# Quantised rows rounded before they are transposed, and laid out by two engines instead of one

## The reference, cut to what matters

```python
def _layernorm(x, axis=-1, eps=1e-05):
    m = jnp.mean(x, axis=axis, keepdims=True)
    v = jnp.var(x, axis=axis, keepdims=True)
    return (x - m) / jnp.sqrt(v + eps)

def fake_quant(x, n_bits=N_BITS):
    qmax = 2 ** (n_bits - 1) - 1
    scale = jnp.maximum(jnp.max(jnp.abs(x)) / qmax, 1e-08)
    q = jnp.clip(jnp.round(x / scale), -qmax - 1, qmax) * scale
    return x + jax.lax.stop_gradient(q - x)

qkv = jnp.einsum('bnc,oc->bno', fake_quant(x), fake_quant(w_qkv)) + b_qkv      # x: the normalised rows
attn = jnp.einsum('bhnd,bhmd->bhnm', fake_quant(q), fake_quant(k)) * scale
```

## Time and profile before

| | value |
|---|---|
| median of three runs | 2032.84 us (2028.87 to 2034.92) |
| span of the profiled execution | 2037.3 us |
| busy: TensorE, VectorE, ScalarE, GpSimd | 74%, 70%, 68%, 57% |
| start of `normalise`'s loop, its last reduction | about 299 us, 423 us |

### The profile page before, as it was taken

One profiled execution on the slowest core, in us unless ns is written; L12 is line 12 of the kernel. 1 busy time (PEld: TensorE's weight loads), 2 busy tenths in 40 slices (PEclk: granted clock), 3 DMA queues, 4 the chain that ended last, 5 costly groups with the idle time before them and its releaser, 6 DMA issues. The chain is left out here.

```text
span 2037.3 us, 49150 instructions
## 1 busy us (share of the span) xinstructions
PE 1498.2 (74%) x12152; PEld 991.7 (49%) x12153; DVE 1431.0 (70%) x3551; ACT 1376.4 (68%) x3956; POOL 1162.3 (57%) x1903
## 2 busy tenths in 40 slices
PE   6999957856656565663688885888865999994663
PEld 6999954411111111111344443555534988884553
DVE  2544559978777777776466666888876777774896
ACT  1323224429999999997799994777753766663885
POOL 2333330046666666662455552677775888884997
PEclk9999978955555555555555555555556999997786
DMA  7654310002222222221544445444433555554785
GB/s 293 258 231 193 160 39 1 1 32 83 85 75 76 76 87 75 84 78 49 136 138 150 143 146 152 132 154 154 154 123 107 140 140 137 146 144 143 224 271 159
DMA packets 184974, 263.32 MB, mean 129 GB/s; under 512 B 28372, under 2 KB 147363, under 8 KB 180328
## 3 DMA queue, kind: packets, MB, share of 16 engines
q1 hardware_dynamic: 137456, 202.16, 31.8%
q0 software_dynamic: 19840, 39.17, 5.4%
q10 hardware_dynamic: 27540, 20.52, 3.1%
HBM read 149.17 MB, written 108.01 MB: 126 GB/s over the span
## 5 line engine op out<-in xcount | busy, mean ns | idle before, releaser
L956 ACT ACTIVATE exps_summed<-s,neg_shift 128x197 f32<-128x197 f32 x1184 | 481.9, 535 | 32.4 <-POOL neg_shift L830 30.4
L956 ACT ACTIVATION_READ_ACCUMULATOR exps_summed<-s,neg_shift (+1 forms) x1184 | 339.0, 317 | 0.0
L993 DVE TENSOR_REDUCE score_max<-s 128x788 f32 (+3 forms) x320 | 285.9, 893 | 66.5 <-PE s L900 58.7
L1353 ACT ACTIVATE exps<-st,scalars 128x788 f32<-128x788 f32 (+1 forms) x320 | 246.4, 891 | 17.6 <-PE st L1262 17.5
L2034 POOL DMA_INDIRECT expert_sums<-y_tile,row_places x216 | 218.4, 1011 | 60.9 <-issue 28.9
L384 PE MATMUL mm<-w_tok,x_transposed 128*128 128x192 f32 x1176 | 209.4, 328 | 0.8 <-ACT x_transposed L345 0.8
L345 ACT COPY x_transposed<-tp 128x768 f32<-128x768 f32 x98 | 78.1, 798 | 176.8 <-PE tp L376 176.8
L384 PEld LDWEIGHTS mm<-w_tok,x_transposed 128*128 128x128 f32 x1176 | 190.8, 192 | 1.2 <-ACT x_transposed L345 1.2
L367 POOL TENSOR_SCALAR x_patches<-x_tile 128x768 f32<-128x768 f32 x98 | 81.4, 831 | 187.7 <-PE tp L376 172.1
L1173 POOL TENSOR_SCALAR probs<-exps 128x788 bf16<-128x788 f32 (+1 forms) x160 | 130.0, 819 | 102.3 <-ACT exps L1353 100.7
L900 PE MATMUL s<-k_int,qk_int 16*128 16x197 bf16 x768 | 98.7, 354 | 108.8 <-ACT exps_summed L956 106.0
(11 more groups left out here) (416 smaller groups left out, 4531.9 us busy)
## 6 DMA issues: line engine op xcount, KB each, us to landing
x_tile<-in_x SPq DMA_DIRECT2D x21, 1792.0 KB, 11.1
z_tile<-listed_rows SPq DMA_DIRECT2D x108, 196.0 KB
v_ints<-v_slots SPq DMA_DIRECT2D x32, 480.0 KB
v_slots_in<-v_ints SPq DMA_DIRECT2D x32, 480.0 KB, 3.6
q_ints<-qk_int SPq DMA_DIRECT2D x32, 295.5 KB
k_ints<-k_int SPq DMA_DIRECT2D x32, 295.5 KB
q_shifted<-q_ints SPq DMA_DIRECT2D x32, 295.5 KB, 3.6
k_ones<-k_ints SPq DMA_DIRECT2D x32, 295.5 KB, 4.3
```

The lines of the kernel that those rows point to most:

```text
L956: act.activation(gone[:, w % 2, k], ps[(turn + w) % 3][:, k, 0:SEQ], ACT.Exp, scale=alpha, bias=nb[:, s, to:to + 1], accum_out=p.lsum[:, b ...
L993: dve.tensor_reduce(columns(m, u), src, op=ALU.max, axis=AXL.X).then_inc(max_done, 1)
L1353: act.activation(ex[:, v % 4, 0:size(u)], src, ACT.Exp, scale=alpha, bias=p.col(C_LNSA)).then_inc(e_ready, 1)
```

## The change

GpSimd gets the rounding: it reads `y` and writes `yr` (`y_rounded`, bf16, two buffers), so TensorE transposes bf16 with the bf16 identity, and PSUM holds bf16. The two parts of a token now go to separate banks: channels 0 to 127 to `pa` as before, channels 128 to 191 to the bank `maxima` in even turns and to the fifth bank of `pq` in odd turns. What is left is plain copies: ScalarE lays out the first part of every turn and the last part of even turns, VectorE the last part of odd turns. ScalarE copies turn t - 2 behind the normalisation of turn t. The doubles and the reductions are the same.

```diff
-        pa = [p.ps(f"pa{k}", [128, 4, 128], F32, c) for k in range(2)]
+        pa = [p.ps(f"pa{k}", [128, 8, 128], BF16, c) for k in range(2)]
...
+        def turned_to(x, rows, t):
+            first = 1 + 4 * t
+            return x[0:rows, :, first:first + 4].rearrange("p b (u e) -> p b u e", e=2)
+
+        def first_channels(t):
+            return pa[t % 2][:, 0:2, :]
+
+        def last_channels(t):
+            b = pq[:, 4] if t % 2 else bank[:]
+            return b[0:D1].bitcast(BF16)[:, 0:2 * ROWS].rearrange("p (u n) -> p u n", u=2)
...
-                for t in range(NG * SIDE // 2):
-                    need(act, t_done, t - 1)
+                def copies(t):
+                    act.wait_ge(t_done, t + 1)
+                    act.copy(turned_to(x0, 128, t), by_image(first_channels(t))).then_inc(x0_act, 1)
+                    if t % 2 == 0:
+                        act.copy(turned_to(x1, D1, t), by_image(last_channels(t))).then_inc(x1_act, 1)
+
+                for t in range(TURNS):
+                    need(act, r_ready, t - 1)
                     for u in range(2):
...
                     ins.then_inc(y_ready, 1)
+                    if t >= 2:
+                        copies(t - 2)
+                copies(TURNS - 2)
+                copies(TURNS - 1)
...
                 pool.wait_ge(ones_ok, 1)
+                for t in range(TURNS):
+                    pool.wait_ge(y_ready, t + 1)
+                    need(pool, t_done, t - 1)
+                    pool.tensor_scalar(yr[:, t % 2], y[:, t % 2], MAGIC, MAGIC, ALU.add, ALU.subtract).then_inc(r_ready, 1)
...
-                    pe.wait_ge(y_ready, t + 1)
-                    need(pe, x_ready, t - 1)
+                    pe.wait_ge(r_ready, t + 1)
+                    need(pe, x0_act, t - 1)
+                    need(pe, x1_dve if t % 2 else x1_act, t // 2)
                     for u in range(2):
-                        nc.tensor.transpose(pa[b][:, u, 0:ROWS], y[:, b, u, 0:128], p.idf[0:ROWS, 0:ROWS])
-                        done = nc.tensor.transpose(pa[b][0:D1, 2 + u, 0:ROWS], y[:, b, u, 128:D], p.idf[0:ROWS, 0:ROWS])
+                        nc.tensor.transpose(first_channels(t)[:, u], yr[:, b, u, 0:128], p.idb[0:ROWS, 0:ROWS])
+                        done = nc.tensor.transpose(last_channels(t)[:, u], yr[:, b, u, 128:D], p.idb[0:ROWS, 0:ROWS])
...
-                        need_apart(pe, x_ready, 7 * (g + 1), tick_t)
-                    need_apart(pe, q_max, ND * g + d - 1, tick_t)
+                        turns = (SIDE // 2) * (g + 1)
+                        pe.wait_ge(x0_act, turns)
+                        pe.wait_ge(x1_act, (turns + 1) // 2)
+                        pe.wait_ge(x1_dve, turns // 2)
+                    need(pe, q_max, ND * g + d - 1)
...
-                def spread(g, w2):
...
-                    for dst, src, rows in ((x0, pa[b][:, 0:2, :], 128), (x1, pa[b][0:D1, 2:4, :], D1)):
-                        first = 1 + 2 * SIDE * g + 4 * w2
-                        ins = dve.tensor_scalar(dst[0:rows, :, first:first + 4].rearrange("p b (u e) -> p b u e", e=2),
-                                                src.rearrange("p u (b e) -> p b u e", e=2), MAGIC, MAGIC, ALU.add, ALU.subtract)
-                    ins.then_inc(x_ready, 1)
+                def odd_turn(t):
                     dve.wait_ge(t_done, t + 1)
+                    dve.tensor_copy(turned_to(x1, D1, t), by_image(last_channels(t))).then_inc(x1_dve, 1)
```

More of the change, by code:

```diff
@@ L441, in normalise @@
         y = p.sb("y", [ROWS, 2, 2, D], F32, c)
+        yr = p.sb("y_rounded", [ROWS, 2, 2, D], BF16, c)
         cy = p.sb("class_y", [128, D], F32, c)
@@ L445, in normalise @@
         mx = p.sb("qkv_max", [128, NG, 5, PAIRS], F32, c)
-        pa = [p.ps(f"pa{k}", [128, 4, 128], F32, c) for k in range(2)]
+        pa = [p.ps(f"pa{k}", [128, 8, 128], BF16, c) for k in range(2)]
         pq = p.ps("pq", [128, 5, 512], F32, c)
         bank = p.ps("maxima", [128, 512], F32, c)
[L449 to L452, removed]
+        (ld, chain, chain_a, red, w_t, w_ok, b_in, b_mv, y_ready, r_ready, t_done, x0_act, x1_act, x1_dve, cls_t,
+         q_done, q_max, red2, eps_ok, max_ok, rows_ok, ones_ok) = p.sems(
+            p.early, "b", "ld chain chain_a red w_t w_ok b_in b_mv y_ready r_ready t_done x0_act x1_act x1_dve cls_t "
+            "q_done q_max red2 eps_ok max_ok rows_ok ones_ok")
         DOUBLES = ([((q, j), (q, j + 1)) for q in range(PAIRS) for j in (0, 2)]
@@ L464, in normalise, with by_image @@
         cw1 = p.cw1
+        TURNS = NG * SIDE // 2
+        def turned_to(x, rows, t):
[6 more added lines that the diff above has]
+            return b[0:D1].bitcast(BF16)[:, 0:2 * ROWS].rearrange("p (u n) -> p u n", u=2)
+        def by_image(v):
+            return v.rearrange("p u (b e) -> p b u e", e=2)
         p.cw0 = cw0
@@ L644, in _ @@
                 dve.sem_inc(w_ok, 1)
-                def spread(g, w2):
-                    t = g * (SIDE // 2) + w2
-                    b = t % 2
+                def odd_turn(t):
                     dve.wait_ge(t_done, t + 1)
-                    for dst, src, rows in ((x0, pa[b][:, 0:2, :], 128), (x1, pa[b][0:D1, 2:4, :], D1)):
-                        first = 1 + 2 * SIDE * g + 4 * w2
-                        ins = dve.tensor_scalar(dst[0:rows, :, first:first + 4].rearrange("p b (u e) -> p b u e", e=2),
-                                                src.rearrange("p u (b e) -> p b u e", e=2), MAGIC, MAGIC, ALU.add, ALU.subtract)
-                    ins.then_inc(x_ready, 1)
+                    dve.tensor_copy(turned_to(x1, D1, t), by_image(last_channels(t))).then_inc(x1_dve, 1)
                 def maxima(g, d):
@@ L664, in _ @@
                     for w2 in range(SIDE // 2):
-                        spread(g, w2)
+                        t = g * (SIDE // 2) + w2
+                        if t % 2:
+                            odd_turn(t)
                         if g:
```

## The result

The changed kernel takes 2078.6 us, median of four runs (2070.86 to 2079.33); the kernel before took 2033.0 on the same chip. The ratio is 1.0222 [1.0202, 1.0242]: slower by 45.6 us, where 10 us faster was predicted and 2032 was the upper end of the range.

What follows compares the result with a forecast made beforehand. VectorE was taken to bound the edited stage. Steady part -12.6, fill +1.5, clock +2.7 and end -2 sum to -10.4 us from the median 2032.84: 2022.4 us; range 2010 to 2032, the forecast's own 2017 to 2027.

Steps and rivals of the forecast that it cites:

- (c): Start of the products: clock low for 7 us, so 2.3 turns instead of 3.8, +2.7 us.
- rival C: Edited stage: TensorE's clock stays or falls low, 3.0 us a turn; all 42 turns give 2070 us; chance 0.06.
- (a): Steady part, 42 turns: 1.85 us a turn instead of 2.15, -12.6 us.
- the coupling stall: Steady part: odd turns wait for VectorE's copy; VectorE idles 3.5 us in 14 turns, giving 1.85 us a turn.
- (b): Fill: ScalarE sets the pace, first product at about 320.9 us instead of 319.34, +1.5 us.
- (d): End of the stage: the dip of the clock is gone, -2 us.
- TensorE's transpositions: Each turn's four transpositions: 0.43 to 0.46 us at the high clock, for bf16 as for f32.
- balance of 1.60 for both engines: Steady part: TensorE and VectorE each need 1.60 us a turn, stalls not counted.
- ScalarE's copies: On ScalarE: 0.28 us of pitch per copy, 0.45 as upper end; costed at nothing in the steady part.
- B: Steady part: ScalarE is the bound; at 0.8 us a copy a turn takes 2.12, total 2038 us; chance 0.06.
- Rival A: Steady part: no stall between engines, or cheaper transposes; VectorE runs at 1.60 us a turn, total 2012; chance 0.23.
- D: Steady part: an unseen buffer wait takes 0.3 us a turn, the gain becomes nil, total 2035 us; chance 0.13.

Runs made afterwards that it cites:

- runs 2: Kernel before with y written and transposed as bf16, layout unchanged and exact rounding left out: 2231.8 us, ratio 1.0165.
- run 4: Changed kernel with GpSimd's rounding written as two additions instead of add and subtract: 2236.8 us, ratio 1.0183.
- run 5: Changed kernel with its bf16 transpositions written as ordinary bf16 products with the identity, f32 results: 2236.7 us, ratio 1.0185.
- run 12: Changed kernel with GpSimd's rounding in two quick multiply-and-add operations, bf16 throughout: 2075.1 us, ratio 1.0199.
- run 11: Changed kernel repeated unedited: 2076.7 us, ratio 1.0212 to the kernel before.
- run 1: Changed kernel with the rounded rows kept and transposed as f32 instead of bf16: 2186.2 us, ratio 0.9956.
- run 7: Changed kernel with turns 0 to 8 as in the kernel before and later turns transposing rounded f32 rows: 2180.5 us, ratio 0.9924.
- run 3: Changed kernel with 24 plain bf16 products of 512 columns, results unused, before the first double: 2197.6 us, ratio 1.0008.
- run 10: Changed kernel with turns 0 to 8 as in the kernel before, later turns bf16, GpSimd's rounding in two quick operations: 2183.8 us, ratio 0.9951.
- run 6: Changed kernel with turns 0 to 8 as in the kernel before, later turns bf16: 2227.3, 2232.3, 2192.2 and 2230.9 us, no ratio formed.

## Why the prediction was wrong, step by step

**(c), the clock, is the step that failed.** It assumed that the products begin with a low stretch like the tail's, 7 us, and rival C, in which all turns are low, had 0.06 on the argument that TensorE would be fuller than before and that a full TensorE at the low clock rose in 410 to 417. The price was about right: 3.06 measured for the 3.0 of a low turn. The argument was not. TensorE was full in after (129 of 130 us) and in runs 2, 4, 5 and 12, and did not rise in the turns. The row of the tail showed products alone; what stands between products was left out of the comparison. The rows now say: low and among bf16 transpositions, it never rose (after and five experiments, run 11 among them); low and among f32 ones, it rose soon behind the first products (run 1) or in the fill (run 7); high, it held under bf16 turns in ten of ten and seven of seven executions (3, 10) and was lost in three of four (6). The one of these three that is profiled lost it at a wait of 1.08 us in front of bf16 turns, stayed low until the turns were over, and run 7 kept it over the same wait in front of f32 ones; whether the shorter wait is what saved run 10 was not tested apart. Why bf16 and f32 differ in all this is not shown. Run 5 excludes the mode of the instruction, and at the low clock both take about the same time: 0.22 to 0.25 each for bf16 (320.58, 320.80, 321.04, 321.26), 0.21 to 0.26 for f32 before.

The Trainium skill, "TensorE: Matmul & The Clock Gate" (Part 4: PE-mode transpose), says of the high clock that it "doesn't engage" for transposes, since such work "doesn't count as PE-busy the same way". For f32 the traces disagree: in before and in run 7 the clock rose in the fill (0.53 and 0.54 in 316 to 318, 1.00 in 318 to 320), on transpositions alone. For bf16 they fit, but ordinary bf16 products with the identity did no better (run 5). The prediction weighed the rule only for the fill, at 2.7 us; carried into the turns, where four of about ten instructions are transpositions, it would have spoken for C.

**(a), the steady part, -12.6.** Right where the clock held, in its mechanism too: run 1 needs 26.04 us for 14 turns, 1.86 a turn, for the 26.0 and 1.85 of the forecast. In its 330 to 400 VectorE waits 7.1 us for TensorE, and TensorE's first transposition of a turn ten times for VectorE's copy (4.3 us), the coupling stall that was forecast. That its total, 10.2 us faster, meets the sum's 10.4 is partly luck, for two errors of the sum offset each other: the fill cost 3.7 us (24.17 against 20.45 from the first normalisation to the first product) instead of 1.5, and the low stretch behind the first product ended after 4 to 5 us instead of 7. In the changed kernel itself the term became +38.2.

**(b), the fill, +1.5.** It was +3.6. The mis-sized term is GpSimd's rounding: 520 ns by interpolation, 1274 as the upper end, 1497 measured. The forecast had ScalarE as the pace; GpSimd was, which is 1.3 of the 2.1 us that were missed (10.9 instead of 9.6 from turn 1 to the first product). The other 0.7 had no term: turn 1 began later, because VectorE's quantising of the weights took longer beside GpSimd's rounding.

**(d), the dip of the tail, -2.** Not in the changed kernel, whose tail starts at 0.50. Run 1 bears it out: 1.00 in 410 to 412, where before had 0.51.

**TensorE's transpositions, 0.43 to 0.46 for bf16 at the high clock.** 0.66 measured (run 3). The estimate halved the 0.92 of four low-clock ones, but it doesn't halve. The forecast's balance of 1.60 for both engines thus holds for f32 alone.

**VectorE's copy, 440 ns**: 445. **ScalarE's copies, 0.28 to 0.45 of pitch**: they last 472 and 466 ns and stand 0.33 apart (320.15, 320.48). ScalarE bounds nothing, B fell. Rival A fell (VectorE idles, run 1), and D too (1.86 a turn, where D had 2.15). C came true; its "four dips of the tail" are four pitches of 1.49 in one dip, and only products stand in it.

**The parts together**, on the experiments' chip: layout alone -10.2, type alone +35.4, both +40.4 (run 4). They don't add to -10 + 35 = 25, because at 0.50 TensorE alone sets the pace and VectorE's relief is worth nothing, while the slower fill of the layout remains.

## What to carry to other kernels

Before the operand type of a TensorE instruction is changed, look at the granted clock of the stage, and compare it only with stretches of the same mixture of instructions: "TensorE is full" was true in every low stretch of turns here. Where a stage is longer by one factor throughout, read the clock column before the waits: here all waits pointed at TensorE and none said why. To test it, put a burst of ordinary products in front of the stage, which costs 7.5 us and tells at once whether the stage can hold what it can't reach.

## What the runs showed of the hardware that was not expected

- The clock has two lasting outcomes for the same turns: 1.00 or 0.50 for all 42 of them, by its state at the start (run 3 against after, run 10 against run 12), and with one kernel it differs between executions, to judge by their times (2192 against 2227 to 2232 us, run 6).
- bf16 transpositions are no cheaper than f32 ones: 0.22 to 0.25 each against 0.21 to 0.26 at the low clock, 0.66 against 0.46 for four at the high one.
- On GpSimd, an addition paired with a subtraction or with a second addition took 1497 ns for 384 elements; pairs of a multiplication and an addition took 514 and 513. Two quick operations beat one slow one.
- A copy of bf16 in runs of four elements cost VectorE 445 ns and ScalarE 466, the same as reading f32 from PSUM cost them (run 1: 453 for VectorE, 464 to 473 for ScalarE).
- VectorE's 128x768 quantising to bf16 took 559 or 560 ns in six profiles with GpSimd idle and 736 to 751 in eight with GpSimd rounding at the same time. Work given to an idle engine slowed the bound one a little, ahead of the loop.
